# Third stage of a two-product graph layer in eleven near-equal outputs, with the residual loaded output by output

## The reference

```python
h = relu(layernorm(x))
s = (adj + adj.T) * 0.5 + eye(N)
d = where(rowsum(s) > 0, rowsum(s) ** -0.5, 0)
y = (Coefficient2 @ (d[:, None] * s * d[None, :])) @ h    # Coefficient2 is adj as well
return x + y
```

## Time and profile before

| | us |
|---|---|
| median of three runs | 178.81 (178.81 to 180.22) |
| profiled execution, device time | 178.74 |
| its span, first to last instruction | 177.0 |
| TensorE busy, first to last matmul | 163.2 |
| before the first matmul | 10.7 |
| after the last matmul | 3.1 |

### The profile page before, as it was taken

How to read it: one execution, slowest core, us unless ns; L and a number is a source line. 1 busy time by engine, 2 the same in 40 slices (tenths; PEclk the granted TensorE clock), 3 DMA queues, 4 the chain that set the end, 5 groups by cost and what they waited for, 6 DMA issues and landing times.

```text
span 177.0 us, 1932 instructions
## 1 busy us (share of the span) xinstructions
PE 163.2 (92%) x704; PEld 130.6 (74%) x704; DVE 84.5 (48%) x141; ACT 77.2 (44%) x134; POOL 29.6 (17%) x55
## 2 busy tenths in 40 slices
PE   0059999999999999999999999999999999999992
PEld 0047888888888888876788888888888888876781
DVE  0577588888889875934135054151340521501101
ACT  2778699999999937822504203032030310300000
POOL 1137835654542500000000000000000000000000
PEclk9999999999999999999999999999999999999999
DMA  5999999999983000000016931010110101101011
GB/s 174 408 415 408 406 413 407 360 354 367 338 256 83 4 0 0 0 0 0 4 34 162 402 147 59 0 63 0 59 59 0 59 4 59 59 0 59 0 34 59
DMA packets 8745, 25.29 MB, mean 143 GB/s; under 512 B 877, under 2 KB 1133, under 8 KB 8737
## 3 DMA queue, kind: packets, MB, share of 16 engines
q1 hardware_dynamic: 8305, 24.49, 37.8%
q10 hardware_dynamic: 432, 0.69, 1.1%
HBM read 22.26 MB, written 2.77 MB: 141 GB/s over the span
## 4 chain that ended last, share of the span: by engine, by line
PE 92%; DMA 3%; DVE 2%; POOL 1%; issue 1%; ACT 0%; SPq 0%; POOLq 0%; DVEq 0%
PE bank L495 92%; DMA AT<-in_adj_t_dram 3%; DVE S L357 1%; ACT g L296 0%; POOL power L222 0%; DVE y_out L448 0%; POOL S L213 0%; SPq L165 0%; DVE g_scale L391 0%; DVE base L366 0%; DVE part_sums L362 0%; DVEq L356 0%; POOLq L221 0%; POOLq L205 0%
## 5 line engine op out<-in xcount | busy, mean ns | idle before, releaser
L495 PE MATMUL bank<-g,ring 128*128 128x512 f32 (+1 forms) x352 | 82.5, 397 | 10.7 <-ACT g L296 10.7
L495 PEld LDWEIGHTS bank<-g,ring 128*128 128x128 f32 (+1 forms) x352 | 65.9, 188 | 26.9 <-issue 10.7
L495 PE MATMUL bank<-z,ring 128*128 128x512 f32 (+1 forms) x352 | 80.8, 391 | 0.0
L495 PEld LDWEIGHTS bank<-z,ring 128*128 128x128 f32 (+1 forms) x352 | 64.7, 184 | 15.9
L303 ACT CAST ring<-AT 128x1408 fp32r<-128x1408 f32 (+1 forms) x11 | 14.6, 1324 | 47.6 <-PE bank L495 47.6
L448 DVE TENSOR_TENSOR y_out<-bank,x_res 128x512 f32<-128x512 f32 (+1 forms) x11 | 7.6, 691 | 52.2 <-PE bank L495 45.3
L431 DVE TENSOR_TENSOR ring<-AT,ring 128x1280 fp32r<-128x1280 f32 (+1 forms) x11 | 15.8, 1440 | 6.0 <-ACT ring L303 6.0
L375 DVE SCALAR_TENSOR_TENSOR S<-S,AT 128x1354 f32<-128x1354 f32 (+1 forms) x11 | 17.2, 1560 | 0.8 <-POOL S L213 0.8
L396 DVE TENSOR_TENSOR ring<-S,ring 128x1024 fp32r<-128x1024 f32 x10 | 12.3, 1227 | 6.9 <-ACT ring L285 6.9
L308 ACT ACTIVATE z<-bank,d_scale 128x512 fp32r<-128x512 f32 (+1 forms) x12 | 7.4, 691 | 14.4 <-PE bank L495 14.4
L213 POOL TENSOR_TENSOR S<-S,eye 128x128 f32<-128x128 f32 x10 | 8.9, 886 | 19.3 <-DMA S<-in_adj_dram 15.0
(11 more groups left out here) (42 smaller groups left out, 37.3 us busy)
## 6 DMA issues: line engine op xcount, KB each, us to landing
AT<-in_adj_t_dram SPq DMA_DIRECT2D x10, 677.0 KB, 6.0
S<-in_adj_dram SPq DMA_DIRECT2D x10, 677.0 KB, 7.4
x_in<-in_x_dram SPq DMA_DIRECT2D x11, 256.0 KB, 4.2
x_res<-in_x_dram SPq DMA_DIRECT2D x1, 2560.0 KB, 9.8
out_dram<-y_out SPq DMA_DIRECT2D x10, 256.0 KB
S<-in_adj_dram ACTq DMA_DIRECT2D x2, 256.0 KB, 4.3
AT<-in_adj_t_dram SPq DMA_DIRECT2D x2, 256.0 KB, 4.9
AT<-in_adj_t_dram SPq DMA_DIRECT2D x1, 507.8 KB, 6.5
```

The costliest lines, as they stand in the source:

```text
L495: return nc.tensor.matmul(dst, stationary, rhs[0:r, parts[1], :], start=first, stop=final)
```

## The change

The third stage still has eleven outputs, but they are seven of 126 rows, two of 110 and two of 126, in order of rows (7 x 126 + 2 x 110 + 2 x 126 = 1354). `THIRD` now lists pairs of first row and size. Everything in the third stage goes by these pairs: the columns of `AT` that are taken, the rows of a bank, `x_res[:, j]` and `y_out[:, j]`. The stages before it are as they were.

The residual is loaded by eleven DMAs, one for each output, where there were two. VectorE still waits for all of them before result 0. Each result is written by one DMA, and there is no cut of the 74 rows into 64 and 10 any more.

```diff
-    T64 = 64
-    THIRD = [*range(NB - 2), NB - 1, NB - 2]
+    WIDE, SLIM = 126, 110
+    sizes = [WIDE] * (NB - 4) + [SLIM] * 2 + [WIDE] * 2
+    assert sum(sizes) == N
+    THIRD = [(sum(sizes[:j]), size) for j, size in enumerate(sizes)]
...
-            i = THIRD[c - C_THIRD]
-            return AT, i * P, cols_of(i)
+            return AT, *THIRD[c - C_THIRD]
...
             sp.wait_ge(chunk_used, C_THIRD - 1)
-            sp.dma_start(x_res[:, 0:FULL, :], x[0:FULL * P, :].rearrange("(k p) d -> p k d", p=P)
-                         ).then_inc(res_done, 16)
-            sp.dma_start(x_res[:, FULL, :], x[FULL * P:NB * P, :]).then_inc(res_done, 16)
-            for j, m in enumerate(THIRD):
+            for j, (row, r) in enumerate(THIRD):
+                sp.dma_start(x_res[0:r, j, :], x[row:row + r, :]).then_inc(res_done, 16)
+            for j, (row, r) in enumerate(THIRD):
                 sp.wait_ge(drained, NB + j + 1)
-                for p0, p1 in ((0, P),) if m < FULL else ((0, T64), (T64, TAIL)):
-                    sp.dma_start(out[m * P + p0:m * P + p1, :], y_out[p0:p1, m, :]).then_inc(out_done, 16)
-            sp.wait_ge(out_done, (NB + 1) * 16)
+                sp.dma_start(out[row:row + r, :], y_out[0:r, j, :]).then_inc(out_done, 16)
+            sp.wait_ge(out_done, NB * 16)
...
             def result(j):
-                m = THIRD[j]
-                r = cols_of(m)
+                _, r = THIRD[j]
                 dve.wait_ge(chunk_used, C_THIRD + j)
-                nc.vector.tensor_tensor(y_out[0:r, m, :], bank[(3 + j) % 8][0:r, :], x_res[0:r, m, :],
+                nc.vector.tensor_tensor(y_out[0:r, j, :], bank[(3 + j) % 8][0:r, :], x_res[0:r, j, :],
                                         ALU.add).then_inc(drained, 1)
...
-            dve.wait_ge(res_done, 32)
+            dve.wait_ge(res_done, NB * 16)
...
-            for j, m in enumerate(THIRD):
+            for j, (_, r) in enumerate(THIRD):
...
-                output(C_THIRD + j, bank[(3 + j) % 8][0:cols_of(m), :], cols_of(m), z, order)
+                output(C_THIRD + j, bank[(3 + j) % 8][0:r, :], r, z, order)
```

## The result

| | before | changed |
|---|---|---|
| median, five runs each | 179.37 | 181.66 |
| lowest to highest | 178.81 to 181.11 | 181.16 to 183.02 |
| ratio to before, 95% interval | | 1.0125 (1.0087 to 1.0163) |
| profiled execution: time, span | 178.74, 177.0 | 183.02, 181.2 |

The changed kernel is 2.2 us slower by the ratio. The forecast had been 178.6 us, in a range of 178.1 to 179.5. The profiled execution of before, 178.74 us, was taken separately and is not one of the five.

What follows compares the result with a forecast made beforehand. The prediction took gapless TensorE matmuls, plus what follows the last one, to bound the kernel. From 178.74 us, -0.45 for shorter matmuls and +0.3 for the end gave 178.6 us, range 178.1 to 179.5.

Steps and rivals of the forecast that it cites:

- What bounds the kernel: Whole kernel: TensorE runs 163.2 us without a gap, so only matmul length and what follows the last matmul can count.
- Length of a matmul at 126 and 110 columns: Third stage: both widths cost what 74 does, 7.288 us an output; ten outputs save 0.045 us each, -0.45 us.
- The three laws: Third-stage spacing: flat up to a knee (taken, 66%), even growth with columns (no change), or a step below 110 (+0.045 us).
- a story of a hidden load that comes in sight: Third stage: weight load hides beside the matmul until too long for its cover, then costs 0.83 ns a column.
- The rival that ended slower: Residual DMAs land after 112.7 us, so TensorE stalls at output 3; 239 us if on 2 engines; 4%.
- The end: After the last matmul: write on 14 engines, ninth row 0.1 us, later first packet 0.2; +0.3 us (+0.1 to +1.15).
- The residual: Third-stage loads: eleven DMAs in place of two, 5 to 10 us of issues, landing at 105.3 us, cost nothing.
- the margin up to 19.6 us: Third stage: residual may land as late as 112.7 us by the old clock before TensorE waits at output 3.
- The chance of 4% for slower by over 1%: Whole kernel: chance of a clear slowdown, given to a residual landing too late for output 3.

Runs made afterwards that it cites:

- run of the new widths alone: Changed kernel, but each residual load takes 128 rows so all 16 DMA engines carry it; ratio 1.0104 (1.0067 to 1.0141), third stage 82.11 us.
- The maps: Two runs of the changed kernel with mixed output widths (96 to 128) and residual loads of 128 rows; outputs of 128 took 7.32 to 7.35 us, no ratio.
- second profile: The changed kernel run once more, unaltered; ratio 1.0096 (1.0062 to 1.013), third stage 82.11 us again.
- first map: Changed kernel with output widths 128, 126, 128, 124, 128, 120, 128, 112, 128, 96, 128 and loads of 128 rows; 126 took 7.47 us, no ratio.
- slim outputs first: Changed kernel with the two outputs of 110 first and the nine of 126 behind them; all eleven took 7.47 us, no ratio.
- slow start avoided: Changed kernel with matmuls of 128 columns in outputs 0 and 1 alone; ratio 1.0051 (1.0023 to 1.008), third stage 81.53 us.
- kernel with full columns and a last write of 128 rows: Changed kernel with 128 weight columns in every third-stage matmul, rows 126 x 7, 110, 108, 126, 128; ratio 1.0027 (0.9998 to 1.0055).
- row of seven 121s: Changed kernel with matmul widths 128, 121 x 7, then 128 three times, loads and last write of 128 rows; ratio 1.0065 (1.004 to 1.0089).

## Why the prediction was wrong

*What bounds the kernel* held: of what the change touches, only the length of a matmul and the end counted, and nothing made TensorE wait.

*Length of a matmul at 126 and 110 columns*, the -0.45 us, is the step that failed, in sign and beyond both of its bounds (-0.55 to +0.045). It measured +1.33 us, alike in two executions of the changed kernel and in the run of the new widths alone. The three laws had one premise in common, that the spacing between the rows at 74 and at 128 lies between their two values. The maps show that it does not. That the excess of 1.4 ns at 128 fitted the slope of the weight load so well, with a knee just at 126, was a coincidence of two points; a story of a hidden load that comes in sight was drawn from them, and 96 columns at 7.47 us, where it gives 7.29, refute it. The rival that ended slower was looked for in the DMAs alone, while the operation that filled 92% of the span was run at two widths that no row showed.

The formula of the Trainium skill, page "TensorE: Matmul & The Clock Gate", section "Back-to-back issue gap", in moving columns alone, gives one spacing for all these matmuls. The section gives it for an isolated matmul (216 ns at 512 columns, an estimate by it), and for a stream of pairs it has a measured 131 ns. The traces have 227 to 233 ns at the same 512 columns, so neither figure holds here.

*The end*, +0.3 us, came near in sum by luck, and was wrong in its parts: it measured +0.43. The write on 14 engines with 9 rows each was forecast. Its data took about 0.5 us more, near the upper bound of 0.55 and not the 0.1 taken; the first packet came 179.17 - 178.37 = 0.80 us after the issue, no later than before, where 0.2 had been added. The two misses partly cancel. The rule for the number of engines, which the Trainium skill states in "DMA: Bandwidth & Descriptors", section "Why a DMA increments its semaphore by 16 and not by 1", agrees with the 14 completion packets.

*The residual* was right in effect. The eleven issues took 5.15 us in all, the lower estimate; it landed 13.6 us into the stage (12.5 in the second profile) where 12.2 had been worked out, and the margin up to 19.6 us was kept. One reading behind the 12.2 was too broad: the old load ran at 409 GB/s with every engine busy only in the middle, and the windows have 139 GB/s from 94 to 96 us and 156 from 102 to 104. The eleven loads never got above 292 GB/s in a window of 2 us.

The sum by trace is then 1.33 + 0.43 = 1.76 us, inside both measured intervals (1.6 to 2.9 and 1.1 to 2.3 us). The chance of 4% for slower by over 1% rested wholly on the residual, and the outcome came by a way that had no chance of its own.

**Open.** The pattern is inherited and depends on how a run of a width begins; what sets it at the entry was not settled. 126 entered from 128 was slow at outputs 0 and 1 and fast at 2 and later; output 0 takes its last two blocks in another order, and both lie beside the residual's transfer, and no run tells these apart. In every trace with 128 columns in output 0, the spacings just ahead of its last one are twice 233 or 234 ns and then 231 or 232, out of the rhythm of the rest; the 126 of the first map was entered right behind them. 126 entered from 110 was fast in the changed kernel, in both its traces, and slow in two others (slim outputs first, slow start avoided). Why 128 had a single level in the third stage of every trace, and what the engine does in the 4 ns, was not seen either. Left over, too, is whether the kernel with full columns and a last write of 128 rows is slower than before at all: 0.5 us by its ratio, with an interval that touches zero, and 0.05 us by its stage.

## What to carry to other kernels

On a path that one engine fills, never fill in the cost of a width between two measured ones: run the one width first, as a single output between the old ones and again as a row of them. Fewer columns of weights mostly cost time here; they bought 0.05 and 0.07 us in single outputs of 74 and 121 columns, and nothing in a row of 121s. Where the rows of an output don't need all 128 columns, loading the full 128 and ignoring the surplus was the faster way (1.0037 against 1.0125 and 1.0096 to the kernel before). Splitting evenly has a second price in the DMAs: 126 rows are carried by 14 engines, and the last write of a kernel pays for that in full, 0.4 us here.

## What was unexpected in the hardware

- The spacing of matmuls with 512 moving columns, in a stream in which each has its own weights, sits at one of a few levels: 226.7, 228.9, 230.0 and 233.3 ns for most widths, as the mean from start to start in the middle of an output. In the third stage 128 columns were always at 228.9, 74 at 226.7, 126 at 230.0 or 233.3, 110 at 233.3, 121 at 226.7 or 230.0, 112, 122, 123 and 124 at 230.0, 96 and 127 at 233.3; 120 (230.1) and 125 (231.2) fit less well.
- A level is the mean of a short cycle of spacings that repeats through an output: 226, 229 and 232 ns at 128 columns, 229 and 231 in the fast 126 of the changed kernel, 231 to 235 in the slow one. In the row of seven 121s the level is 230.0 throughout, and six of them take 7.41 us for four slower matmuls at their start (about 233, 234, 257 and 240 ns).
- The level is inherited. The same five outputs of 126 columns took 7.47 us each or 7.37 us each, by whether two outputs ahead of them had 126 or 128 columns. The changed kernel's levels were the same in both of its traces, and in the trace of its widths alone.
- A 126-row write on 14 engines took 1.3 us for its data, a 128-row write on 16 engines 0.8: over half as long again for an eighth more rows an engine, and so in the writes beside matmuls too. A packet took 99 ns in place of 86 in the last write, which explains only part of it.
